# q and k transposed as row halves in two shared banks, P's transposes joined, and the engines' lists reordered

## What is computed

```python
q, k, v = split(shift_token(x) @ wqkv)         # 8 heads of 64
q, k = rotary_xpos(l2norm(q) * qs, l2norm(k) * ks)
sim = 8 * q @ k.T                              # windows of 128, keys of this and the last window
x = x + (softmax(mask(sim)) @ v) @ wo
h = layernorm(shift_token(x)) @ w1 + b1        # 2 * 682 columns
x = x + (a * gelu(g)) @ w2 + b2
```

## Time and profile before

| | |
|---|---|
| median of 3 runs | 2842.33 us |
| profiled execution: time, span | 2843.03 us, 2840.9 us |
| TensorE, DVE, ScalarE, POOL busy | 96%, 82%, 81%, 58% of the span |
| mean granted TensorE clock | 0.986 |
| bytes moved by DMA | 166.99 MB, mean 59 GB/s |

### The profile page before, as it was taken

How to read it: one execution, slowest core, us unless ns; L and a number is a source line. 1 busy time by engine, 2 the same in 40 slices (tenths; PEclk the granted TensorE clock), 3 DMA queues, 4 the chain that set the end, 5 groups by cost and what they waited for, 6 DMA issues and landing times.

```text
span 2840.9 us, 79380 instructions
## 1 busy us (share of the span) xinstructions
PE 2729.4 (96%) x29124; PEld 2438.8 (86%) x29124; DVE 2324.6 (82%) x6459; ACT 2288.0 (81%) x5557; POOL 1639.0 (58%) x1652
## 2 busy tenths in 40 slices
PE   7999947899999999999999999999999999999998
PEld 6888846788888888888888888888888888888888
DVE  3979977888888888888888787888888888888884
ACT  4979956788888888888888787888888888888885
POOL 2323316666666666666666565666666666666663
PEclk9999978999999999999999999999999999999999
DMA  3252111111111121111111213111111111111111
GB/s 101 65 187 72 40 60 50 58 54 50 56 54 50 54 58 57 52 52 54 56 48 53 83 57 104 51 49 47 50 47 47 50 48 50 50 50 50 50 39 46
DMA packets 211349, 166.99 MB, mean 59 GB/s; under 512 B 21522, under 2 KB 206612, under 8 KB 209940
## 3 DMA queue, kind: packets, MB, share of 16 engines
q1 hardware_dynamic: 139284, 127.82, 14.8%
q10 hardware_dynamic: 71680, 34.10, 4.1%
HBM read 110.89 MB, written 42.58 MB: 54 GB/s over the span
## 4 chain that ended last, share of the span: by engine, by line
PE 84%; DVE 8%; issue 2%; ACT 2%; DMA 2%; SPq 1%; POOL 1%; ACTq 0%; DVEq 0%; POOLq 0%
PE ps L431 31%; PE ps L430 18%; PE ps L397 10%; PE ps L494 7%; PE ps L510 6%; PE ps L526 4%; PE ps L479 3%; DVE Sm L1212 3%; PE ps L536 2%; DVE Ar L1183 1%; PE ps L562 1%; PE ps L457 1%; DVE oTl L1235 1%; DMA oF<-ro_scratch 1%; PE ps L384 1%
## 5 line engine op out<-in xcount | busy, mean ns | idle before, releaser
L826 ACT ACTIVATE Sm<-Sm,nb 128x256 f32<-128x256 f32 (+1 forms) x1024 | 502.9, 496 | 1.3 <-DVE nb L1212 0.5
L1212 DVE CUSTOM_DVE_ANT_0 Sm<-ps,mask,sc 128x256 f32<-128x256 f32 (+1 forms) x1024 | 420.5, 476 | 56.7 <-issue 27.1
L1386 POOL TENSOR_TENSOR rs<-rs,mhalf 128x8 f32<-128x8 f32 x256 | 422.6, 1651 | 14.0
L1474 POOL TENSOR_TENSOR uTl<-Gl,uTh 128x512 fp32r<-128x512 f32 (+1 forms) x192 | 212.1, 1104 | 331.8 <-ACT uTh L900 211.3
L430 PE MATMUL ps<-zTh,W1h 128*128 128x256 f32 (+1 forms) x1408 | 377.9, 290 | 0.0
L430 PE MATMUL ps<-zTh,W1l 128*128 128x256 f32 (+1 forms) x1408 | 365.9, 282 | 0.0
L806 ACT ACTIVATE sq<-ps 128x512 f32<-128x512 f32 x256 | 151.7, 592 | 256.3 <-PE ps L431 252.7
L1284 DVE SCALAR_TENSOR_TENSOR Gl<-ps,vecs,Gl 128x256 f32<-128x256 f32 (+1 forms) x384 | 172.0, 475 | 222.4 <-PE ps L430 152.8
L431 PE MATMUL ps<-WQh,hTh 128*128 128x512 f32 x768 | 340.7, 444 | 2.7 <-ACT hTh L800 2.7
L431 PE MATMUL ps<-WQl,hTh 128*128 128x512 f32 x768 | 304.2, 396 | 0.0
L1485 POOL TENSOR_TENSOR Ar<-Ar,Br 128x512 f32<-128x512 f32 x128 | 164.6, 1286 | 206.7 <-DVE Br L1185 206.6
(11 more groups left out here) (190 smaller groups left out, 8677.0 us busy)
## 6 DMA issues: line engine op xcount, KB each, us to landing
oF<-ro_scratch ACTq DMA_DIRECT2D x256, 128.0 KB, 3.1
tb<-tab SPq DMA_DIRECT2D x128, 128.0 KB, 2.3
xc<-x SPq DMA_DIRECT2D x32, 256.0 KB, 3.0
rwkv_scratch<-rw SPq DMA_DIRECT2D x32, 256.0 KB, 2.7
rk<-rwkv_scratch SPq DMA_DIRECT2D x64, 128.0 KB, 2.3
xin<-x SPq DMA_DIRECT2D x64, 128.0 KB, 2.3
x_scratch<-x SPq DMA_DIRECT2D x64, 128.0 KB, 1.7
y_scratch<-os SPq DMA_DIRECT2D x64, 128.0 KB, 4.2
```

The source lines that it names most:

```text
L826: act.activation(Sm[:, h, c0:c1_], Sm[:, h, c0:c1_], ACT.Exp, bias=nb[:, h:h + 1], scale=-1.0, accum_out=sm[:, n % 2, h:h + 1]).then_inc(S ...
L1212: dve.tensor_tensor_reduce(Sm[:, h, c0:c1_], PS[:, bank["scores", n, q, h % 2], (h // 2 % 2) * 256 + c0:(h // 2 % 2) * 256 + c1_], mask[:, ...
L1386: return pool.tensor_tensor(ap, ap, mhalf[:, 0:ap.shape[-1]], ALU.pow)
L1474: pool.tensor_tensor(uT[1][:, j, :], Gl[:, g, :], uT[0][:, j, :].bitcast(F32), ALU.subtract).then_inc(S["ul"], 1)
```

## The change

`turn_qk` is called once for a unit, directly behind the scores, and transposes k and q in one run of 16 transposes of 64 rows by 64 columns. Rows 0 to 63 go to one bank and rows 64 to 127 to another, and each bank holds k in its upper half of columns and q in its lower. The copies `qk_hi` and `qk_lo` wait for the whole run and read both banks (by one instruction where the banks are neighbours, by two elsewhere). `turn_p` 0 and 1 stand side by side in both steps. pv and wo of the even step's list move to the end of the odd step's list, behind the v projection, for the same unit. pre stands ahead of hT in even steps.

```diff
@@ -57,7 +57,7 @@
 U = 2 * NG
 NY, NV, NX = 8, 5, 7
 STEPS1 = NCH + 5
-STEPS2 = U + 13
+STEPS2 = U + 14
 PK, PV, PR, PT1 = 0, 2, 4, 6


@@ -327,6 +320,21 @@

     return PS[:, bank:bank + 2, :].rearrange("p b (g t) -> p (b g) t", g=2)

+def halves(n):
+
+    return sorted((bank["qkT", n, 0], bank["qkT", n, 1]))
+
+def turned(n, i):
+
+    lo, hi = halves(n)
+    pieces = [(lo, 0, 2)] if hi == lo + 1 else [(lo, 0, 1), (hi, 1, 2)]
+    for k, r0, r1 in pieces:
+        yield (PS[:, k:k + r1 - r0, i * 256:i * 256 + 256].rearrange("p r (c t) -> p c r t", t=64),
+               slice(r0, r1))
+
+def by_half(t):
+    return t.rearrange("p c (r t) -> p c r t", r=2)
+
 def read_out(user):
     if user is None:
         return S["end"], 3
@@ -350,7 +358,7 @@
     if what == "qkv":
         return (S["v"], n + 1) if i[0] == 2 else (S["rope"], 2 * n + (2, 1)[i[0]])
     if what == "qkT":
-        return S["qkl"], 2 * n + (2, 1)[i[0]]
+        return S["qkl"], 2 * n + 2
     if what == "hT":
         return S["hTl"], n + 1
     return S["x1"], n + 1
@@ -468,17 +476,20 @@
                lambda a, c: WQ[a][:, c, i * 512:(i + 1) * 512],
                lambda: w.wait_ge(S["hTl"], n + 1)).then_inc(S["p2"], 1)

-def turn_qk(n, i):
-    k = bank["qkT", n, i]
-    if i:
-        w.wait_ge(S["kn"], n + 1)
-    else:
-        w.wait_ge(S["qr"], n + 1)
-    w.wait_ge(*read_out(former["qkT", n, i]))
-    for c in range(4):
-        ins = pe.transpose(PS[:, k, c * 128:(c + 1) * 128],
-                           Ar[:, i * 512 + c * 128:i * 512 + (c + 1) * 128], ident[:, :])
-    ins.then_inc(S["p3"], 1)
+def turn_qk(n):
+
+    w.wait_ge(S["kn"], n + 1)
+    w.wait_ge(S["qr"], n + 1)
+    for r in range(2):
+        w.wait_ge(*read_out(former["qkT", n, r]))
+    banks = halves(n)
+    for i in (1, 0):
+        for c in range(4):
+            for r in range(2):
+                rows = slice(64 * r, 64 * r + 64)
+                ins = pe.transpose(PS[:, banks[r], i * 256 + c * 64:i * 256 + c * 64 + 64],
+                                   Ar[rows, i * 512 + c * 128:i * 512 + (c + 1) * 128], ident[rows, rows])
+        ins.then_inc(S["p3"], 1)

 def scores(n, q):
     c0, c1_ = cols(n)
@@ -607,42 +618,32 @@
         return 0 <= t - d < U

     if t % 2 == 0:
-        if live(6):
-            pv(t - 6, 0)
-            pv(t - 6, 1)
-        if live(7):
-            wo_mm(t - 7)
         if live(11):
             mlp((t - 11) // 2, 0)
+            mlp((t - 11) // 2, 1)
         if live(5):
             turn_p(t - 5, 0)
-        if live(11):
-            mlp((t - 11) // 2, 1)
-        if live(5):
             turn_p(t - 5, 1)
         if live(11):
             mlp((t - 11) // 2, 2)
         if live(4):
             scores(t - 4, 0)
             scores(t - 4, 1)
+        if live(3):
+            turn_qk(t - 3)
         if live(2):
             qkv(t - 2, 1)
         if live(5):
             turn_r(t - 5)
-        if live(3):
-            turn_qk(t - 3, 1)
         if live(2):
             qkv(t - 2, 0)
-        if live(3):
-            turn_qk(t - 3, 0)
-        if live(2):
             qkv(t - 2, 2)
+        if live(0) and t < NG:
+            pre_mm(t)
         if live(1):
             turn_h(t - 1)
         if live(10):
             turn_z(t - 10)
-        if live(0) and t < NG:
-            pre_mm(t)
     else:
         if live(6):
             pv(t - 6, 0)
@@ -653,29 +654,30 @@
             turn_z(t - 10)
         if live(13):
             w2_mm(t - 13)
-        if live(5):
-            turn_p(t - 5, 0)
         if live(12):
             w2_mm(t - 12)
         if live(5):
+            turn_p(t - 5, 0)
             turn_p(t - 5, 1)
         if live(4):
             scores(t - 4, 0)
             scores(t - 4, 1)
+        if live(3):
+            turn_qk(t - 3)
         if live(2):
             qkv(t - 2, 1)
         if live(5):
             turn_r(t - 5)
-        if live(3):
-            turn_qk(t - 3, 1)
         if live(2):
             qkv(t - 2, 0)
-        if live(3):
-            turn_qk(t - 3, 0)
-        if live(2):
             qkv(t - 2, 2)
+        if live(5):
+            pv(t - 5, 0)
+            pv(t - 5, 1)
         if live(1):
             turn_h(t - 1)
+        if live(6):
+            wo_mm(t - 6)
         if live(0) and t < NG:
             pre_mm(t)

@@ -813,10 +815,12 @@
                    ACT.Copy).then_inc(S["v"], 1)

 def qk_hi(n, i):
-    w.wait_ge(S["p3"], 2 * n + (2, 1)[i])
+    w.wait_ge(S["p3"], 2 * n + 2)
     w.wait_ge(S["p4"], 4 * (n - 1) + 4)
     dst = kT[0][:, n % 2, :, :] if i else qT[0][:, :, :]
-    act.activation(flat(dst), PS[:, bank["qkT", n, i], :], ACT.Copy).then_inc(S["qkh"], 1)
+    for src, r in turned(n, i):
+        ins = act.activation(by_half(dst)[:, :, r, :], src, ACT.Copy)
+    ins.then_inc(S["qkh"], 1)

 def exp(n, q):
     c0, c1_ = cols(n)
@@ -1195,11 +1196,13 @@
     dve.tensor_scalar(rs[:, n % 2, :], ss[:, :], 1e-24, None, ALU.max).then_inc(S["rsm"], 1)

 def qk_lo(n, i):
-    w.wait_ge(S["qkh"], 2 * n + (2, 1)[i])
+    w.wait_ge(S["qkh"], 2 * n + 2)
     w.wait_ge(S["p4"], 4 * (n - 1) + 4)
     hi, lo = ((kT[a][:, n % 2, :, :] if i else qT[a][:, :, :]) for a in (0, 1))
-    dve.tensor_tensor(flat(lo), PS[:, bank["qkT", n, i], :], flat(hi).bitcast(F32),
-                      ALU.subtract).then_inc(S["qkl"], 1)
+    for src, r in turned(n, i):
+        ins = dve.tensor_tensor(by_half(lo)[:, :, r, :], src, by_half(hi)[:, :, r, :].bitcast(F32),
+                                ALU.subtract)
+    ins.then_inc(S["qkl"], 1)

 def masked_max(n, q):
     c0, c1_ = cols(n)
```

More of the change, by code:

```diff
@@ L141, in psum_order2 @@
             yield "zT", t - 10
-        if live(0) and t < NG:
-            yield "pre", t
     else:
@@ L913, in scalar_program @@
                         gelu((t - 11) // 2, 0)
+                        u_hi((t - 11) // 2, 0)
+                        gelu((t - 11) // 2, 1)
                     if live(5):
@@ L923, in scalar_program @@
                     if live(11):
-                        u_hi((t - 11) // 2, 1)
                         gelu((t - 11) // 2, 2)
@@ L927, in scalar_program @@
                         oT_hi(t - 6)
+                    if live(3):
+                        qk_hi(t - 3, 1)
+                        qk_hi(t - 3, 0)
+                    if live(11):
+                        u_hi((t - 11) // 2, 1)
                     if live(2):
@@ L967, in scalar_program @@
                         oT_hi(t - 6)
+                    if live(3):
+                        qk_hi(t - 3, 1)
+                        qk_hi(t - 3, 0)
                     if live(2):
                         square(t - 2, 1)
-                    if live(0) and t < NG:
-                        pre_norm(t)
                     if live(5):
                         rT_out(t - 5)
-                    if live(3):
-                        qk_hi(t - 3, 1)
                     if live(2):
@@ L979, in scalar_program @@
                         store_r(t - 5)
-                    if live(3):
-                        qk_hi(t - 3, 0)
+                    if live(0) and t < NG:
+                        pre_norm(t)
+                    if live(4):
+                        exp(t - 4, 0)
                     if live(2):
                         v_out(t - 2)
-                    if live(4):
-                        exp(t - 4, 0)
                     if live(5):
                         load_r(t - 5)
-                    if live(1):
-                        hT_hi(t - 1)
         def vector_program(dve):
@@ L1303, in vector_program @@
                 if t % 2 == 0:
+                    if live(11):
+                        glu((t - 11) // 2, 0)
                     if live(9):
                         z_norm(t - 9)
+                    if live(5):
+                        o_sums(t - 5)
+                    if live(11):
+                        glu((t - 11) // 2, 1)
+                        glu((t - 11) // 2, 2)
+                    if live(4):
+                        masked_max(t - 4, 0)
+                        masked_max(t - 4, 1)
+                    if live(3):
+                        qk_lo(t - 3, 1)
+                    if live(7):
+                        zero_h2(t - 7)
+                    if live(3):
+                        qk_lo(t - 3, 0)
+                    if live(1) and t - 1 < NG:
+                        pre_y(t - 1)
+                    if live(6):
+                        oT_lo(t - 6)
+                    if live(2):
+                        rope(t - 2, 1)
+                        rope(t - 2, 0)
+                else:
+                    if live(12):
+                        u_tail((t - 12) // 2)
+                    if live(3):
+                        sums(t - 3)
+                    if live(2):
+                        hT_lo(t - 2)
+                    if live(1) and t - 1 < NG:
+                        pre_x1(t - 1)
                     if live(8):
@@ L1510, in gpsimd_program @@
                 if t % 2 == 0:
```

(22 more changed lines are left out.)

119 lines of the change are left out of this document (33 added, 86 removed).

## The result

The changed kernel takes 2813.55 us (median of 4 runs, 2810.15 to 2814.85), beside 2842.24 for the kernel before on the same chip: a ratio of 0.9899, interval 0.9885 to 0.9913. It is faster by 28.7 us, not by 71, and lies 1.6 us above the range that was given.

A forecast was written before the change was run, and what follows sets the result against it. TensorE was taken to bind (2729.4 of 2840.9 us busy). Terms: -72 for saved work, +3 fill, -12 old waits, +10 new waits, -71 in all: 2771 us from 2842.33, range 2747 to 2812.

The forecast's parts named there:

- TensorE's price: TensorE work saved per unit: 0.25 us for q and k, 0.31 for P; 0.56 in 128 units, 72 us.
- P's own row for the half-row transposes: Sixteen q/k transposes behind the scores priced like P's (16 in 0.52 us): 0.55 taken, between 0.52 and 1.44.
- near 35.0: Sign of being right: TensorE's pair in layer 1 near 35.0 us, from 36.19 before.
- rival 1: All of the gain arrives, no new waits, 4 us more for fewer switches: 2757 us; chance 0.14.
- old waits: Even step's pre waiting for rotary products: 0.5 us in each of 25 waits, 12 us, gone with pre ahead of hT.
- the new waits: Odd step's pv in layer 0 waits for DVE's k rope: 0.4 us in 25 pairs, 10 us; layer 1 nothing.
- hide a landing of 3 us: Layer 1 table loads queued behind POOL's later final additions: POOL's new list hides their landing, no cost taken.
- one step more at the end holds only POOL's work: End of the run: the added step has no work but POOL's; only 3 us lost, in the fill.
- Rival 2: PSUM readers become the bound of layer 0 and touch layer 1: 1.0 us lost in 32 pairs, 2803; chance 0.15.
- Rival 3: ScalarE's P copies in odd steps hold up q and k: 1.5 us in 64 pairs, 2867, slower; chance 0.06.
- Rival 4: Half transposes of q and k don't overlap: 1.44 us instead of 0.52, 115 us more, 2886; chance 0.02.
- The marks that were set: Signs: TensorE near 96% busy, sixteen transposes in 0.5 to 0.65 us, P visit about 1.15, pre's wait found at pv.

The follow-up runs named there:

- run 9: Changed kernel with DVE's one-column copy of hT put ahead of q's rope and POOL's final additions back in the odd step: 2760.47 us, 0.9711.
- run 10: Changed kernel with DVE's hT column copy early, POOL's final additions in the odd step and the read of line 1299 ahead of z_norm: 2758.61 us, 0.9706.
- run 1: Changed kernel with DVE's reads of line 1299 (the down projections) moved ahead of z_norm in the odd list: 2828.1 us, 0.9949.
- run 11: Kernel before with only DVE's carried column of hT copied ahead of q's rope: 2840.07 us beside 2843.84, 0.9988.
- run 12: Kernel before with P in one run in both steps and DVE's hT column copied early: 2816.5 us, 0.9904.
- run 5: Kernel before with only P put in one run, in both steps and for the readers of P: 2853.68 us, 1.0034.
- run 8: Changed kernel with DVE's 0.14 us copy of hT's carried column moved from behind the sums to ahead of q's rope: 2771.34 us, 0.9754.
- edit 2: POOL's final additions moved back to the odd step; alone on the changed kernel 2807.25 us, 0.9875.
- run 6: Kernel before with only q and k transposed as row halves in one run behind the scores, their copies moved to fit: 2845.22 us, 1.0009.

## Why the prediction was right or wrong

**TensorE's price: right in its parts, too low by a fifth.** By starts, from the last pair of scores to the second product of the v projection: 1519.89 to 1524.22 before, 4.33 us, and 1130.02 to 1133.96 after, 3.94. That is 0.39 a unit for q, k and the row sums' transpose together, or 0.37 with the median of the `Ar` visits, 0.61; the sum had 0.25, and nothing for the row sums' 0.08. P: two visits of 0.64 with 0.09 in and 0.10 out each, 1.66, became one of 1.14 with the same ends, 1.33; 0.33, for 0.31 forecast. Together 0.70 a unit, 1.40 a pair, 90 us in 128 units, where the sum had 72. That TensorE's busy time fell by just 72.3 is partly chance: busy adds up lengths as the profile models them, and the price was made of start distances. Taking P's own row for the half-row transposes (0.55, between 0.52 and 1.44) was the right choice, and going from scores into transposes of the same form costs nothing, as taken.

**Pairs.** Without waits, layer 0 would be 37.96 less 1.40 and less the old wait of 0.28, 36.28; layer 1 36.19 less 1.40, 34.79. Run 9 measured 36.23 and 34.90. So the start distances price the work to 0.1 us a pair in both layers (in layer 1 with an odd P visit of 1.26 us in run 9, where the sum has 1.02, so something else there came out shorter), and the forecast's "near 35.0" for layer 1 is what run 9 shows. That rival 1's 2757 lies so near runs 9 and 10 (2760 and 2759) is luck in part: its work is 14 us too low (76 for 90), and its old waits and its ends are 5 and 11 too good.

**The step that failed: the new waits.** The prediction had "0.4 us in each of 25 pairs: 10 us" at pv, and nothing for layer 1, since "its DVE has 7 us of room". Measured are 37.13 less 36.28, 0.85, and 35.62 less 34.79, 0.83, so 0.84 in 64 pairs, 54 us. Room in busy time says nothing on an engine whose instructions wait for one another in a loop: DVE was idle for 4.6 and 6.3 us in the two pairs and still handed over a 0.14 us copy too late. The prediction followed the PSUM banks to their readers, and one bank right (k's rope is next in line, as run 1 shows, with 0.9). It never followed the semaphores between ScalarE and DVE. The gate on DVE's column was there to be seen in the kernel before: 40.9 us of ScalarE's idle time, which cost 1 to 6 us in all (run 11). The prediction took 1.1 us out of TensorE's pair and never asked which waits between other engines had been hidden behind its work. Run 12 against run 5 shows that the gate costs 37 us already with P's part of the change alone and DVE's list of before; run 8 shows 42 in the whole change.

**The transfers.** The prediction let the table loads behind POOL's final additions "hide a landing of 3 us": it looked at the table loads and their user on POOL. The price lay elsewhere: SyncE's list piles up behind its output stores, and a small store of ScalarE's lands late. The trace points to it, and 10.9 us between runs 8 and 9 bear it out, for POOL's additions and the transfers together.

**Fill and drain.** From the first to the last row-sum transpose the time went from 2325.9 to 2283.4 us, 42.5 less: 90 gross and some 7 of old waits, less 54. The first stands 6.6 us later (459.6 to 466.2), and what follows the last is 7.7 longer (55.4 to 63.1): 14 us, where the prediction had 3 for the fill and "one step more at the end holds only POOL's work". It holds MLP parts too, and in the chain that ended last stands

```profile
2753.51 4.07 DMA ro_scratch<-r
```

which before took 1.19 us and with edit 2 takes 1.76. The fill carries TensorE's 8.7 us in 2 waits for POOL's `Ar` (0.7 before). Neither was tried by itself, and each of these landings is a single value; run 9 still has both ends (6.6 and 5.3 us), so most of this belongs to the new stages and stays with them.

**The miss as a sum.** 71 forecast against 28 measured: the gross gain 18 better (90 for 72), old waits 5 worse (7 for 12), new waits 44 worse (54 for 10), ends 11 worse (14 for 3): 42 worse.

**The rivals.** Rival 2 came nearest with 2803, and in kind: waits that the relaid lists add, in both layers, though with the time worked out as 1.0 us in 32 pairs. But its mechanism, readers of PSUM short of time, isn't what bound: run 8 leaves DVE's work as it is, and the wait goes. The prediction set beside it the Trainium skill, TensorEngine Tiling (Array Packing), PSUM Bottleneck, by which the evacuation may be the bound once packing has made TensorE faster; the waits at first looked like it (DVE's read of line 1299), and the pairs of run 9, with TensorE idle for 0.07 us, show that it isn't so here. Rival 3 had the right engine and the wrong gate: ScalarE's queue did hold P, through a column copy and a transfer and not through its P copies. Rival 4 fell with the 0.59 us.

**The marks that were set.** Met: no P copies of ScalarE and no sums of DVE as releasers in layer 1, the sixteen in 0.5 to 0.65, a visit to P of 1.14 in the even step, no wait of pre for the rotary products. Missed: 94% busy and not 96, 35.6 in layer 1, nothing at pv. The mark for "TensorE doesn't bind", waits over 40 us in the second stage, was passed: the run's list has 39.0 and 16.7 in the two new waits' rows, where the first had 16.0 before.

**Open.** What delays the scores behind the odd step's P by 0.27 us in run 12, and by 0.24 in layer 1 of run 9; how much of the column's 42 us the relaid lists add to what a shorter TensorE list alone would lose; whether the column also held run 6; how the 14 us at the ends divide; whether the 0.24 us by which pre's low part starts late in even steps of layer 0 in the kernel after costs anything of its own.

## What to carry to other kernels

When work is taken out of the engine that binds, look first at the waits that the *other* engines have for one another in the kernel before: they may be free only while the binding engine is slower. Here ScalarE stood 40.9 us for a DVE copy of 0.14 us, at a cost of 4 us; with P's visits joined and the lists as they were the same gate cost 37 us, in the whole change 42, and moving one instruction took it away. Such a small instruction, behind a longer block on its own engine and ahead of another engine's work, is to be priced by what waits for it and not by its length. When an instruction waits for two others, the row may name the wrong one: compare the ends of both with the start. A releaser in the list of waits can be the last link of a loop through other engines: if bringing it forward moves the wait instead of removing it (run 1), follow the lateness back to the first instruction that stood ready but not issued. Price an engine's saved work by start distances, and test it by a stretch in which nothing waits (run 9), since the two parts tried alone gained nothing while their sum was worth 90 us.

## What had not been expected of the hardware

- Sixteen half-row transposes, alternating between the two row halves, took 0.59 us, 0.037 each by starts; the eight full ones that turn the same elements took 0.84, 0.105 each. So a full one costs more than two halves (0.074).
- The start behind the row sums' transpose (a product into 8 rows) came 0.03 us later when a projection's product followed, and 0.10 when full transposes did.
- A 4 KB store took 1.19 us to land in the drain of the kernel before, 1.76 with edit 2, and 4.07 in the kernel after; in the step of layer 1 above, its readers were issued 4.7 us behind it, with eight loads on another engine's queue just ahead.
- The idle time that a row gives is less than what the starts lose: 0.62 listed where the scores start 0.79 late (1108.59 to 1109.50, less 0.12), and 0.65 where P's halves lie 0.84 further apart (1.36 for 0.52).
